# Two gather sums of a four-layer graph network: quads with counted visits before, the first layer's fixed visits after

## The reference, cut to what matters

```python
# third graph layer
x = h @ W.T + b
x = norm * x
msg = x[src]
agg = jax.ops.segment_sum(msg, dst, num_segments=h.shape[0])
return agg * norm
# fourth graph layer
out = jax.ops.segment_sum(norm[:, None] * h[src], dst, num_segments=N) + b
```

## Time and profile before

| what | time |
|---|---|
| median of three runs | 5332.52 us |
| the profiled execution, span | 5709.5 us |
| third layer's gather sum, in the profile | 3682 to 4265 us |
| fourth layer's gather sum, in the profile | 4880 to 5475 us (its first gather at 4887.7 us) |
| second layer's gather sum (not changed) | 1703 to 2318 us |

### The profile page before, as it was taken

The page is one execution under the profiler, slowest core; times in us unless marked ns, Lnnn a source line. Parts: engine busy times, 40 slices in busy tenths (PEclk is TensorE's granted clock), DMA queues, the critical chain, the costliest instruction groups (busy, mean ns, idle before and its releaser), DMA issues. The chain is left out here.

```text
span 5709.5 us, 67954 instructions
## 1 busy us (share of the span) xinstructions
PE 4142.4 (73%) x19769; PEld 3142.0 (55%) x19769; DVE 2438.6 (43%) x4746; ACT 1163.7 (20%) x2671; POOL 2168.6 (38%) x2090
## 2 busy tenths in 40 slices
PE   5788884654816666799976999455559999555668
PEld 2555553443614444599975888333437677334445
DVE  4577778877234444356655000421223222212244
ACT  1233330001220000232322444100004333000023
POOL 0566654554436666000000210466650000566621
PEclk9888887996958888899986999677779999777789
DMA  2677874530743223210012998233330000233310
GB/s 77 208 243 241 250 215 151 162 98 23 235 128 88 85 86 86 86 38 8 7 41 82 336 323 281 89 88 93 87 97 26 1 1 16 75 91 88 91 37 23
DMA packets 375879, 639.34 MB, mean 112 GB/s; under 512 B 73053, under 2 KB 270072, under 8 KB 375424
## 3 DMA queue, kind: packets, MB, share of 16 engines
q1 hardware_dynamic: 275262, 342.97, 18.4%
q0 software_dynamic: 100288, 292.14, 17.6%
HBM read 526.37 MB, written 108.57 MB: 111 GB/s over the span
## 5 line engine op out<-in xcount | busy, mean ns | idle before, releaser
L2554 PE MATMUL sum_ps<-gathered_rows,hit 128*125 (+1 forms) x3328 | 1061.5, 477 | 842.0 <-issue 561.2
L2468 POOL DMA_INDIRECT gathered_rows<-k_table,index x1176 | 1160.8, 987 | 1281.1 <-ACT index L2457 717.6
L2554 PEld LDWEIGHTS sum_ps<-gathered_rows,hit 128*125 128x125 f32 (+1 forms) x3328 | 744.9, 235 | 1158.0 <-issue 1033.1
L97 POOL DMA_INDIRECT rows_all<-kv_table,src_of_visit x416 | 448.5, 1078 | 310.6 <-issue 135.5
L2538 DVE TENSOR_TENSOR node_sums<-node_sums,sum_ps 125x256 f32 x244 | 102.3, 419 | 918.0 <-DMA composed<-in_L_gnn_b 495.7
L2457 ACT ACTIVATE index<-src_of_chunk 128x4 int32<-128x4 int32 x294 | 59.2, 205 | 1647.0 <-DMA gathered_rows<-k_table,index 1581.1
L777 PE MATMUL ps_q<-q,hit_t 125*128 x832 | 322.5, 473 | 5.9 <-issue 5.2
L1057 PE MATMUL ps_sum<-summand,hit 128*125 128x261 f32 x832 | 211.6, 397 | 147.1 <-DVE odd_sums L1017 123.2
L2538 DVE TENSOR_TENSOR window_sums<-window_sums,sum_ps 126x256 f32 x344 | 144.8, 421 | 348.2 <-PE sum_ps L2554 183.0
L2762 PE MATMUL qk_ps<-window_sums,composed 128*128 128x126 f32 (+1 forms) x2400 | 292.1, 279 | 0.0
L1996 DVE TENSOR_TENSOR y<-out_ps,b 128x256 f32<-128x256 f32 x120 | 50.9, 424 | 551.2 <-PE out_ps L1895 464.0
(11 more groups left out here) (478 smaller groups left out, 6714.6 us busy)
## 6 DMA issues: line engine op xcount, KB each, us to landing
w<-in_L_ffn_W SPq DMA_DIRECT2D x112, 1024.0 KB
v_kept<-rows_all SPq DMA_DIRECT2D x104, 512.0 KB
v_rows<-v_kept SPq DMA_DIRECT2D x104, 512.0 KB, 3.6
gathered_rows<-k_table,index POOLq DMA_INDIRECT x1176
w<-in_L_ffn_w SPq DMA_DIRECT2D x64, 256.0 KB
b<-in_L_ffn_b SPq DMA_DIRECT2D x88, 128.0 KB
y_slots<-y SPq DMA_DIRECT2D x32, 256.0 KB
y_slots<-y SPq DMA_DIRECT2D x56, 128.0 KB
```

The source lines that it names most:

```text
L97: pool.indirect_dma_start(env.ring[:, k % KEPT_RING, i, :], None, env.kv_table, bass.IndirectOffsetOnAxis(env.src_of_visit[:, k * VB + i:k ...
L2468: pool.indirect_dma_start(self.rows[:, (q % SLOTS) * CHUNKS + c, :], None, self.table, bass.IndirectOffsetOnAxis(self.index[:, q % SLOTS, ...
L2554: mm = pe.matmul(sum_ps[0:rows, k % banks, 0:D], hit[:, g % (lead + 1), i * chunks + c, :], gather.rows[:, ds(first[i] + c, 1), :].rearran ...
```

## The change

- `visit_sum_phase` takes the place of the two runs of `gather_sum_phase` on quads. It sums by the first layer's 416 visits. POOL fetches the 128 rows of each visit itself, with `src_of_visit` as the index, into place `b % 8` of a ring of eight batches (32 chunks). Every wait is for a constant. ACT copies no indices and SP counts nothing.
- TensorE makes one product per visit into a bank of its own, with fixed addresses and no registers. VectorE makes the `hit` matrices once per batch of four visits (500 columns, as before) and adds once per visit, so 416 times; the visit's tile still comes from a table through a register, now read right behind the previous add.
- `setup_phase` keeps three tables aside in HBM in place of one, and `relation_router_phase` loads three in place of one. The quads' tables now live only in `setup_phase`; the window sum of the second layer is as it was.

```diff
@@ setup_phase, SP
+                sp.wait_ge(tabled, 1)
+                sp.dma_start(env.tile_of_visit_kept, env.tile_of_visit[:]).then_inc(kept, 16)
                 sp.wait_ge(read, 2)
-                sp.dma_start(env.quad_key_kept, quad_key[:]).then_inc(kept, 16)
-                sp.wait_ge(kept, 16)
+                sp.dma_start(env.src_of_visit_kept, env.src_of_visit[:]).then_inc(kept, 16)
+                sp.dma_start(env.rel_dst_kept, env.rel_dst[:]).then_inc(kept, 16)
+                sp.wait_ge(kept, 48)
                 sp.wait_ge(x_landed, 16)
@@ relation_router_phase, SP
-                sp.dma_start(env.quads.key[:], env.quad_key_kept).then_inc(key_landed, 16)
+                sp.dma_start(env.tile_of_visit[:], env.tile_of_visit_kept).then_inc(key_landed, 16)
+                sp.dma_start(env.src_of_visit[:], env.src_of_visit_kept).then_inc(key_landed, 16)
+                sp.dma_start(env.rel_dst[:], env.rel_dst_kept).then_inc(key_landed, 16)
...
@@ new
+class VisitGather:
+    def gpsimd(self, pool):
+        for b in range(VT // VB):
+            if b >= RING:
+                pool.wait_ge(self.multiplied, (b - RING + 1) * VB)
+            for i in range(VB):
+                k = b * VB + i
+                pool.indirect_dma_start(self.rows[:, b % RING, i, :], None, self.table, bass.IndirectOffsetOnAxis(
+                    self.env.src_of_visit[:, k:k + 1], 0)).then_inc(self.env.gathered[b % RING], 16)
+
+def visit_sum_phase(env, table, sums, clear):
...
+            @block.vector
+            def _(v):
+                def hits(b):
+                    make_hits(v, env, hit[:, b % (lead + 1)], env.rel_dst, P, b).then_inc(hits_made, 1)
+
+                def tile_of(k):
+                    return v.value_load(env.tile_of_visit[0:1, k:k + 1], min_val=0, max_val=T - 1)
...
+                tile = tile_of(0)
+                for b in range(batches):
+                    if b > 0:
+                        v.wait_ge(multiplied, b * VB)
+                    if b + lead < batches:
+                        hits(b + lead)
+                    for i in range(VB):
+                        k = b * VB + i
+                        v.wait_ge(multiplied, k + 1)
+                        if k > 0:
+                            v.wait_ge(summed, k)
+                        here = sums[:, ds(tile, 1), :].rearrange("p o c -> p (o c)")
+                        v.tensor_tensor(here, here, sum_ps[0:P, k % banks, 0:D], ALU.add).then_inc(summed, 1)
+                        if k + 1 < VT:
+                            tile = tile_of(k + 1)
+
+            @block.tensor
+            def _(pe):
+                for b in range(batches):
+                    pe.wait_ge(hits_made, b + 1)
+                    pe.wait_ge(env.gathered[b % RING], gather.landed(b))
+                    for i in range(VB):
+                        k = b * VB + i
+                        if k >= banks:
+                            pe.wait_ge(summed, k - banks + 1)
+                        pe.matmul(sum_ps[0:P, k % banks, 0:D], hit[:, b % (lead + 1), i, :], gather.rows[:, b % RING, i, :],
+                                  start=True, stop=True).then_inc(multiplied, 1)
@@ build
-            gather_sum_phase(env, env.k_table, env.src_of_chunk, env.quads, env.node_sums, P, 1)
+            visit_sum_phase(env, env.k_table, env.node_sums, True)
             wide_tail_phase(env)
-            gather_sum_phase(env, env.k_table, env.src_of_chunk, env.quads, env.node_sums, P, 1, False)
+            visit_sum_phase(env, env.k_table, env.node_sums, False)
             small_tail_phase(env)
```

More of the change, by code:

```diff
@@ L187, in setup_phase @@
     with ExitStack() as st:
+        env.quads = Visits(env, st, "quads", P, T, 1, False)
         rows_i = sb(env, st, "rows_i", [QUADS, 4, CHUNKS, CH], I32)
@@ L212, in setup_phase @@
         made, step, masked, compared, selected, read = [ph.sem() for _ in range(6)]
-        counted, tiled, chunk_values, window_values, turned = [ph.sem() for _ in range(5)]
+        counted, tiled, chunk_values, window_values, turned, tabled = [ph.sem() for _ in range(6)]
         names = ["dst", "src", "edge_type_6", "edge_type_64"]
@@ L312, in _ @@
                     done(v.tensor_copy(tiles[0:1, 0:visits], tile_bc[j][0:1, :]))
+                    if out is None:
+                        v.sem_inc(tabled, 1)
                     if out is not None:
@@ L1571, in _ @@
                     sp.dma_start(rows_of(env.token_table, g), env.rows[:, g * GT:(g + 1) * GT, :]).then_inc(tokens_stored, 16)
-                sp.wait_ge(key_landed, 16)
+                sp.wait_ge(key_landed, 48)
                 sp.wait_ge(tokens_stored, 16 * G)
@@ L2557, in _, with __init__, landed @@
                         mm.then_inc(multiplied, 1)
+class VisitGather:
+    def __init__(self, env, st, ph, table, multiplied):
+        self.env, self.table, self.multiplied = env, table, multiplied
+        self.rows = sb(env, st, "visited_rows", [128, RING, VB, D])
+        self.base = list(env.gathered_base)
+        for s in range(RING):
+            env.gathered_base[s] += 16 * VB * len(range(s, VT // VB, RING))
+    def landed(self, b):
+        return self.base[b % RING] + 16 * VB * (b // RING + 1)
+    def gpsimd(self, pool):
[6 more added lines that the diff above has]
+                    self.env.src_of_visit[:, k:k + 1], 0)).then_inc(self.env.gathered[b % RING], 16)
@@ new lines, in visit_sum_phase, with _ @@
+def visit_sum_phase(env, table, sums, clear):
+    nc = env.nc
+    ph = Phase(env)
+    lead, banks = 3, 8
+    batches = VT // VB
+    half = T // 2
+    with ExitStack() as st:
+        multiplied = ph.sem()
+        gather = VisitGather(env, st, ph, table, multiplied)
+        hit = sb(env, st, "hit", [128, lead + 1, VB, P])
+        sum_ps = ps(env, st, "sum_ps", [128, banks, 512])
+        cleared, hits_made, summed = [ph.sem() for _ in range(3)]
+        with nc.Block() as block:
+            @block.sync
+            def _(sp):
+                ph.clear_other()
+            @block.gpsimd
+            def _(pool):
+                gather.gpsimd(pool)
+            @block.scalar
+            def _(act):
+                if clear:
+                    act.activation(sums[:, half:T, :], env.ones[0:P, 0:1].unsqueeze(2).to_broadcast([P, T - half, D]),
+                                   ACT.Copy, scale=0.0).then_inc(cleared, 1)
+            @block.vector
[4 more added lines that the diff above has]
+                    return v.value_load(env.tile_of_visit[0:1, k:k + 1], min_val=0, max_val=T - 1)
+                for b in range(lead):
+                    hits(b)
+                if clear:
+                    v.memset(sums[:, 0:half, :], 0.0).then_inc(cleared, 1)
+                    v.wait_ge(cleared, 2)
+                tile = tile_of(0)
[24 more added lines that the diff above has]
+                                  start=True, stop=True).then_inc(multiplied, 1)
@@ L3324, in build @@
         env.part = sb(env, st, "part", [128, 1])
-        env.quads = Visits(env, st, "quads", P, T, 1, False)
         env.pairs = Visits(env, st, "pairs", WN, NW, 2, True)
         env.src_of_chunk = sb(env, st, "src_of_chunk", [128, QUADS, CHUNKS], I32)
-        env.quad_key_kept = nc.dram_tensor("quad_key_kept", (128, env.quads.visits, CHUNKS), F32).ap()
+        env.tile_of_visit_kept = nc.dram_tensor("tile_of_visit_kept", (1, VT_PAD), I32).ap()
+        env.src_of_visit_kept = nc.dram_tensor("src_of_visit_kept", (128, VT_PAD), I32).ap()
+        env.rel_dst_kept = nc.dram_tensor("rel_dst_kept", (128, VT_PAD), F32).ap()
         env.k_table = nc.dram_tensor("k_table", (N, D), F32).ap()
@@ L3366, in build @@
         env.x = sb(env, x_stack, "x", [P, T, D])
-        env.quads.key = sb(env, x_stack, "quads_key", [128, env.quads.visits, CHUNKS])
+        visit_tables(env, x_stack)
         with ExitStack() as f1:
```

8 lines of the change are left out of this document (5 added, 3 removed).

## The result

The changed kernel takes 5397.0 us in the median (5385.5 to 5399.3, 4 runs), the kernel before 5332.7 us beside it (5324.9 to 5343.8, 4 runs): a ratio of 1.0109, 95% interval 1.0091 to 1.0126, so 1.1% slower. The forecast was 5392 us.

What follows compares the result with a forecast made beforehand. The prediction took POOL's beat of 1.28 us per gather to bound both sums. Without stalls in the timed runs, 2 x 28.8 + 2 = +60 us on 5332.5 us gave 5392 us, range 5252 to 5412.

Steps and rivals of the forecast that it cites:

- Points 1, 3, 6: POOL's gathers in each sum: 24 more for +31 us, no wait for indices -0.7, fewer hits -2.
- Point 3: Start of each sum: the first gather no longer waits for ACT's 0.49 us of indices, -0.7 us.
- Point 6: Gathers beside VectorE's hits: 18 fewer hits, -2 us a sum; other bound +71 us if adds were as bad.
- Points 4 and 5: Both sums: TensorE's 832 passes and VectorE's 416 adds stay hidden under POOL's pace, no cost.
- the fourth case: VectorE becomes the bound or its adds slow POOL: at 1.45 us per visit +200 us, 5532 us; chance 0.05.
- Point 2: POOL's stalls behind TensorE's stretched register instructions: -71 and -66 us in the profile, zero in timed runs without stalls.
- The 377 us: Profiled span 5709.5 us against timed 5332.5 us, taken as a sign that the stalls are the profiler's, three to one.
- the stalls are real: Rival: the two sums' stalls are in the timed runs too, so the change gives 5255 us; chance 0.22.
- Point 7: End of each sum: four adds follow the last products, 0 to +0.9 us, taken as +0.5.
- Point 8: Setup: SP stores one table more, behind the first store; 0 to +7.4 us, taken as +2.
- Point 9: Relation router: two large tables loaded in place of one, SP free before its token store; 0, at most +6 us.
- first case: No stalls in the timed runs, 24 gathers more in each sum: 5392 us, range 5368 to 5412; chance 0.64.

Runs made afterwards that it cites:

- e2: The changed kernel with each of the two sums stopped after 392 of its 416 gathers: 5331.4 us, ratio 0.998 to the kernel before.
- e3: The kernel before with 24 spare gathers, which nothing reads, added in each of the two quad sums: 5419.1 us, ratio 1.0138.
- e1: The kernel before, unchanged, timed and profiled once more: 5341.7 us, ratio 1.0001; the profiled execution is 5340.0 us long.
- e6: The changed kernel with hit matrices made only for the first four batches of each sum and then used again: 5365.5 us, ratio 1.0054 to the kernel before.
- e5: The changed kernel with VectorE's adds cut from 256 to 32 columns: 5391.6 us, ratio 1.0104 to the kernel before.
- e13: The changed kernel, unchanged, run once more in the second condition: 5866.5 us against 5684.5 for the kernel before, ratio 1.033.
- e12: The kernel before, unchanged, profiled once more, in the second condition: 5686.9 us, profile span 5685.1 us.
- e7: The changed kernel with its hit matrices made on ScalarE in place of VectorE: 5366.1 us, ratio 1.0052 to the kernel before.
- e11: The changed kernel with the hit's row of column numbers read from PSUM in place of SBUF, second condition: 5864.0 us against 5684.8, ratio 1.0322.
- e8: The kernel before with the hits of all three gather sums made on ScalarE and gather indices taken without ACT's copies: 5294.6 us, ratio 0.9915.

## Why the prediction was right, and where it was wrong

The time and the direction were right, and the term that decides the sum, 24 gathers at POOL's pace, is shown by e2 and e3. The explanation of the first profile's stalls, on which it had put its odds, was wrong. That the forecast came true was therefore in part luck: it holds because the comparison was made in the first condition. In the second the same change costs 182 us in place of 64.

- **Points 1, 3, 6: the gathers.** Forecast +28.8 us a sum, of it 31 for 24 gathers; measured +28.4 and +27.2. The first-to-last span of 532 us was forecast and is 532.1 and 532.3. e2 shows that with 392 gathers nothing of the loss is left, e3 that 24 gathers alone make it. Point 3's -0.7 us didn't come: from VectorE's first hit of the phase to POOL's first gather it is 0.68 us in e1 and 0.61 us after, and in the fourth layer's sum 0.68 and 0.59. Point 6 gave -2 us for fewer hits: e6 has 0.12 us a hit, so 18 fewer are -2.1. Its other bound, +71 us if an add were as bad as a hit, is shut out by e5.
- **Points 4 and 5: TensorE and VectorE hidden.** Right in the first condition: no long gap, adds 0.83 us apart, idle time between batches. In the second the fourth case came true: VectorE's chain of adds is the bound, though held up by its sequencer and not by the adds' own length. That case was priced at 1.45 us per visit and +200 us in all; measured are, in e13's fourth sum from the first gather (4962.1) to the end of the last add (5626.2), 664.1 / 416 = 1.60 us per visit, and +182 us against that condition's before. It had been given 0.05 because of the 0.92 us between adds in the earlier trace rows. But there VectorE had 122 visits' register work, in the changed kernel it has 416.
- **Point 2: the stalls.** The step "that looks like something that is written for every instruction, and that is the profiler's" failed. e1 has the profiler and no stretching, e12's seven neighbours have no profiler and the time of a stretched run. The Trainium skill's "NOTIFIC — the notification-queue block" (7.1, Overflow) says that the block's internal path for records always holds its producers back rather than lose a record. No run here shows that at work. That the timed comparison had no stalls was true for another reason, that the machine was in the first condition.
- **Point 2's price in the profile,** -71 and -66 us with the stalls, was wrong as well. It took the register work off TensorE and didn't ask where it went: the adds' tile loads went from 122 to 416 on VectorE. In the second condition the change costs +66 and +71 us in the sums, where the sum on record, with the gathers counted in, had -42 and -37 us. The rival "the stalls are real", at 5255 us, therefore has the wrong sign even where the stalls are real.
- **The 377 us** were a sound warning, wrongly read. In e12, 345 us longer than e1, the two sums hold 61 us each, the second layer's sum 90 and the first layer 83, though TensorE's arithmetic isn't stretched there. The prediction looked for the rest in the same kind of row and took its absence for a sign of the profiler. What the first layer does have is the pauses of TensorE shown under e12.
- **Point 7:** +0.5 forecast; 7.4 us against 7.6, so nothing. **Point 8:** +2 forecast, +0.7 measured. **Point 9:** 0 forecast, and nothing measured: SP is free at 2796 us, ahead of its store of tokens at 2808, and all that lies ahead of the first gather of the third layer's sum takes 0.7 us less. The 2.4 us more between the two sums lie behind that phase and aren't explained.
- **The first case's range.** The bounds of points 1, 8 and 9 add up to 5374 to 5414 us, where the text has 5368 to 5412. Nothing hangs on it.

The prediction also weighed the Trainium skill's "SBUF — State Buffer" (Who interferes with whom), which infers that a VectorE instruction with two inputs in SBUF leaves descriptor generation alone. For these gathers e6, e7 and e11 disagree: 975 ns a gather with such hits, 947 without, 947 with them on ScalarE, 948 with one input in PSUM. The same section has such an instruction get in the way of what GpSimd reads from SBUF, and a gather's index lies there; whether that read is what is held up wasn't tested.

Open are: what puts the machine in the second condition; what holds an engine's sequencer up in it, and whether that goes with register instructions or with the number of instructions of any kind; and why it shows as pauses between rows in the first layer, which is 83 us longer there.

## What to carry to other kernels

When a phase runs at the pace of one engine's instructions, count them first: 24 more gathers at 1.28 us decided this change where the engine's pace was undisturbed, and no cheaper wait beside them could matter. When the profiled execution is much longer than the timed runs, don't explain the gap: run the same kernel again before you believe either. And when work is taken off an engine that stalls, ask which engine has it now, and whether that one would stall in the same way. A median and a maximum aren't enough to name a stall: the least duration, and the rows beside it, told here that more than the arithmetic was held up.

## What the runs showed of the hardware

- An indirect gather of 128 rows of 1 KB takes POOL 0.945 us and 0.30 us to the next one (e8). A VectorE comparison with two inputs in SBUF makes a gather that meets it longer, as the 1.19 us in the earlier trace rows, but not each: it is 0.12 us per comparison in the mean. Eight times narrower adds, with one input in PSUM, changed a sum of 532 us by at most 1 us (e5), and hits with one input in PSUM left the gather at 0.948 us (e11).
- The same program had two steady times, 5333 to 5343 us and 5685 us, 6.5% apart, both with and without the profiler. In the longer one the sequencer of one engine goes, mostly for 2 to 20 us at a time, by rows of close to 0.70 us or a few ns, waits and register instructions (0.151 us otherwise) alike: TensorE's in the gather sums of the kernel before, VectorE's in the changed ones. In the first layer TensorE stands still for 2.8 to 5.1 us twelve times instead (e12).
- The ratio of two kernels isn't the same in both: 1.0109 and 1.033 for the change, 0.9915 and 1.0031 for e8's.
